# First loads and projections reordered, and every fourth head of layer 0 masked behind its exponentials by GpSimd, in a two-layer gated attention kernel

## What is computed

```python
scores = jnp.einsum('bhqd,bhkd->bhqk', Q, K) / scale
scores = jnp.where(mask, scores, NEG_INF)          # -1e10
attention = jax.nn.softmax(scores, axis=-1)
heads_out = jnp.einsum('bhqk,bhkd->bhqd', attention, V)
```

## Time and profile before

| | |
|---|---|
| median of 3 runs | 1293.08 us (1290.47 to 1293.56) |
| the profiled execution's own time | 1296.06 us |
| its span, first to last instruction | 1294.8 us |
| mean granted TensorE clock | 0.984 of full |
| TensorE busy | 1212.6 us |
| VectorE busy | 894.7 us |
| ScalarE busy | 710.4 us |
| GpSimd busy | 480.4 us |

### The profile page before, as it was taken

One profiled execution on the slowest core, in us unless ns is written; L12 is line 12 of the kernel. 1 busy time (PEld: TensorE's weight loads), 2 busy tenths in 40 slices (PEclk: granted clock), 3 DMA queues, 4 the chain that ended last, 5 costly groups with the idle time before them and its releaser, 6 DMA issues.

```text
span 1294.8 us, 25126 instructions
## 1 busy us (share of the span) xinstructions
PE 1212.6 (94%) x9236; PEld 858.0 (66%) x9236; DVE 894.7 (69%) x2680; ACT 710.4 (55%) x1197; POOL 480.4 (37%) x675
## 2 busy tenths in 40 slices
PE   6799999999999989999999989999999999888998
PEld 5466667666776664444448866676676776577987
DVE  2678767886777646589999956767868777642333
ACT  1355555555655548889983326666566665622221
POOL 5344333443343100057000434343643643322555
PEclk8899999999999999999999999999999999988999
DMA  5422334233432032000003644364464342137983
GB/s 158 140 79 82 109 92 128 80 87 107 121 104 67 11 97 84 1 1 1 1 1 124 198 138 116 99 161 136 135 170 123 117 137 61 51 144 230 312 198 39
DMA packets 121941, 137.22 MB, mean 106 GB/s; under 512 B 12881, under 2 KB 116427, under 8 KB 121797
## 3 DMA queue, kind: packets, MB, share of 16 engines
q1 hardware_dynamic: 111888, 125.98, 32.9%
q0 software_dynamic: 7296, 8.15, 3.5%
q10 hardware_dynamic: 2634, 1.49, 0.4%
HBM read 58.42 MB, written 27.36 MB: 66 GB/s over the span
## 4 chain that ended last, share of the span: by engine, by line
PE 56%; DVE 6%; issue 3%; ACT 2%; DMA 1%; POOL 1%; SPq 1%; ACTq 0%; POOLq 0%; DVEq 0%
PE PS L641 14%; PE PS L687 5%; PE PS L444 5%; PE PS L384 5%; PE PS L427 4%; PE PS L655 4%; PE PS L403 4%; PE PS L502 2%; PE PS L696 2%; PE PS L476 2%; PE PS L391 2%; DVE NM L1086 1%; PE PS L520 1%; PE PS L485 1%; ACT P L808 1%
## 5 line engine op out<-in xcount | busy, mean ns | idle before, releaser
L808 ACT ACTIVATE P<-PS 128x512 f32<-128x512 f32 x512 | 302.2, 601 | 165.0 <-PE PS L430 98.3
L1083 DVE CUSTOM_DVE_ANT_0 MX<-PS,NQ 128x256 bf16<-128x256 f32 x512 | 192.5, 418 | 66.9 <-PE PS L403 66.6
L427 PE MATMUL PS<-QS,KS 99*128 99x256 bf16 x1024 | 225.7, 274 | 8.1 <-ACT P L808 7.1
L1086 DVE TENSOR_REDUCE NM<-PS 128x2 f32<-128x512 f32 x256 | 173.6, 685 | 75.9 <-PE PS L403 71.4
L403 PE MATMUL PS<-KS,QS 96*128 96x256 bf16 x1024 | 196.8, 275 | 23.4 <-DVE NM L1083 15.1
L403 PEld LDWEIGHTS PS<-KS,QS 96*128 96x128 bf16 x1024 | 87.0, 98 | 89.0 <-DVE NM L1083 28.2
L444 PE MATMUL PS<-P,V 128*32 128x256 f32 x2048 | 137.0, 385 | 1.5 <-ACT P L808 1.5
L427 PEld LDWEIGHTS PS<-QS,KS 99*128 99x128 bf16 x1024 | 95.2, 99 | 53.9 <-ACT P L808 20.5
L430 PE MATMUL PS<-NK,identb 128*128 128x256 bf16 x512 | 126.9, 273 | 0.0
L641 PE MATMUL PS<-XNT,wup 128*128 128x512 f16 x576 | 124.9, 379 | 0.0
L641 PEld LDWEIGHTS PS<-XNT,wup 128*128 128x128 f16 x576 | 56.2, 98 | 67.4
(11 more groups left out here) (233 smaller groups left out, 2476.1 us busy)
## 6 DMA issues: line engine op xcount, KB each, us to landing
KS<-PP SPq DMA_DIRECT2D x192, 128.0 KB, 2.9
QS<-PP SPq DMA_DIRECT2D x192, 128.0 KB, 2.4
WH<-in_wex SPq DMA_DIRECT2D x16, 768.0 KB
WG<-in_wex SPq DMA_DIRECT2D x10, 768.0 KB
bufd<-bias_row SPq DMA_DIRECT2D x5, 1032.0 KB, 12.2
XB<-in_x SPq DMA_DIRECT2D x16, 256.0 KB, 2.9
CT<-in_ctxT SPq DMA_DIRECT2D x16, 256.0 KB, 3.1
x1d<-XB SPq DMA_DIRECT2D x16, 256.0 KB, 2.1
```

The lines of the kernel that those rows point to most:

```text
L427: ins = tensor.matmul(o, t.KS[b % 3][0:99, h, 128 * kt:128 * kt + 128], t.QS[b % 3][0:99, h, :], start=True, stop=(L == 1))
L808: scalar.activation(t.P[h % 8][:, :, :], PS[:, h % 2, :].rearrange("p (k n) -> p k n", k=2), ACT.Exp).then_inc(s_ex, 1)
L1083: ins = vector.tensor_tensor_reduce(t.MX[:, 2 * (h % 2) + qt, :], PS[:, bk, 256 * qt:256 * qt + 256], t.NQ[b % 4][:, qt, :], -1.0, 1.0e30, ...
L1086: ins = vector.tensor_reduce(nm[:, :, h], PS[:, bk, :].rearrange("p (t n) -> p t n", t=2), X, ALU.max, negate=True)
```

## The change

Masking. In layer 0 heads 0, 4, 8 and 12 no longer get the penalty matmuls on their transposed scores. Instead `pe_marks` sums the penalties NK of all keys by a matmul with ones, `dve_marks` makes from this and the mask bytes a tile MK of ones and zeros (ones where a key counts, and for a query that has none), and `pool_mask` on GpSimd limits the exponentials to 1 and multiplies them with MK, at slots 1, 7, 9 and 13. `pe_av` waits for it (s_pm). There are three buffers MK; loading a mask also waits for the marks of the batch before the last.

First loads. SyncE issues rows, mask and context of batches 0 and 1 and rows and mask of batch 2 in one burst; the context of batch 2 comes at (-2, 14). Norms of batches 0 and 1 both run in s = -3. Batch 0's rows are transposed before its keys are projected. The casts and low pieces of batch 1's queries move from the sixth to the ninth slot of its head work, their stacks behind them. Twelve warming matmuls stand before the values of batch 0. ScalarE's bias loads and rows of ones come at (-1, 0), GpSimd's gated biases and the bias additions of batches 0 and 1 at (-1, 5) and (-1, 6), its clearing of V before the first slot.

Beside these, semaphores are merged (s_z and s_num into s_iv, d_cr into d_i, d_wr into d_ql) and w_r lies in unused columns of AM. The diff, cut to its core:

```diff
@@ -126,6 +126,18 @@
+def masked_after(L, h):
+    return L == 0 and h % 4 == 0
+def mark_at(s, k):
+    if (s, k) == (-3, 5):
+        return 0
+    return s + 2 if k == 14 and 1 <= s + 2 < NB else None
@@ -134,6 +146,32 @@
+def norms_at(L, s, k):
+    if s == -3:
+        steps = [(0, k + 6)] + ([(1, k + 3)] if L == 0 else [])
+    else:
+        steps = [(s + 3, k)] if s + 3 < NB and (L, s) != (0, -2) else []
+    return [(b, kk) for b, kk in steps if 6 <= kk <= 10]
+def loads_at(L, s, k):
+    return k == 2 and (L, s) not in ((0, -2), (0, -1))
+def mid_at(L, b):
+    return 8 if (L, b) == (0, 1) else 5
+def rows_first(L, b):
+    return (L, b) == (0, 0)
@@ -233,7 +272,7 @@
         w_s = tile(m, "w_s", [128, 48], F32)
-        w_r = tile(m, "w_r", [128, 48], F32)
+        w_r = AM[:, 48:96]
@@ -416,17 +456,18 @@
         def pe_scores_t(L, b, h):
...
             i = 16 * n + h
-            pe.wait_ge(d_i, 48 * (L + 1))
+            pe.wait_ge(d_i, 16 + 48 * (L + 1))
...
             pe.wait_ge(s_ex, i - 1)
-            if L == 0:
+            if L == 0 and not masked_after(L, h):
...
                 o = PS[:, bk, 256 * kt:256 * kt + 256]
+                on_scores = L == 0 and not masked_after(L, h)
                 ins = tensor.matmul(o, t.KS[b % 3][0:99, h, 128 * kt:128 * kt + 128], t.QS[b % 3][0:99, h, :],
-                                    start=True, stop=(L == 1))
-                if L == 0:
+                                    start=True, stop=not on_scores)
+                if on_scores:
@@ -436,6 +477,8 @@
             pe.wait_ge(s_ex, 16 * n + 4 * g + 4)
+            if L == 0:
+                pe.wait_ge(s_pm, 4 * b + g + 1)
@@ -445,6 +488,15 @@
+        def pe_marks(b):
+            bk = odd_bank(("mk", b), s_mk, b + 1)
+            pe.wait_ge(s_cst, 1)
+            pe.wait_ge(s_pen, b + 1)
+            for kt in range(2):
+                ins = tensor.matmul(PS[:, bk, 0:256], onesb[:, :], t0.NK[b % 4][:, kt, :], start=(kt == 0), stop=(kt == 1))
+            ins.then_inc(s_mc, 1)
@@ -547,13 +599,15 @@
                     continue
+                if kk == (0 if rows_first(L, b) else 1):
+                    pe_xn(L, b)
...
                     pe_keys(L, b)
-                if kk == 1:
-                    pe_xn(L, b)
...
                 if kk == 13:
+                    if (L, b) == (0, 0):
+                        pe_warm(5, 12)
@@ -577,6 +631,8 @@
                     pe_ranks(GROUP_OF[s - 2][0])
+            if L == 0 and mark_at(s, k) is not None:
+                pe_marks(mark_at(s, k))
@@ -782,21 +838,24 @@
+        def spread(v, n):
+            return v.rearrange("(o n) -> o n", o=1).broadcast_to([128, n])
+        def act_biases():
+            scalar.dma_start(bias_row[:, 0, :], spread(a["b0"], D)).then_inc(s_g, 16)
+            scalar.dma_start(bias_row[:, 1, :], spread(a["b1"], D)).then_inc(s_g, 16)
         def act_setup():
-            def spread(v, n):
-                return v.rearrange("(o n) -> o n", o=1).broadcast_to([128, n])
...
             scalar.dma_start(gates[:, 2:4], spread(a["g_ffn"], 2)).then_inc(s_g, 16)
-            scalar.dma_start(bias_row[:, 0, :], spread(a["b0"], D)).then_inc(s_g, 16)
-            scalar.dma_start(bias_row[:, 1, :], spread(a["b1"], D)).then_inc(s_g, 16)
-            act.wait_ge(s_g, 64)
+            act.wait_ge(s_g, 32)
...
             act.wait_ge(s_cr, 1)
-            scalar.dma_start(crd, XNf[0:3, 0:2048]).then_inc(d_cr, 16)
+            scalar.dma_start(crd, XNf[0:3, 0:2048]).then_inc(d_i, 16)
         def act_ones(L):
-            act.wait_ge(d_cr, 16)
+            act.wait_ge(d_i, 16)
@@ -904,10 +963,10 @@
                     continue
+                if kk == (0 if rows_first(L, b) else 1):
+                    act_xt(L, b)
...
                     act_split(L, b, 0)
-                if kk == 1:
-                    act_xt(L, b)
@@ -1010,8 +1069,10 @@
         def act_program():
             act_setup()
-            act_ones(0)
             for s, k in slots(0):
+                if (s, k) == (-1, 0):
+                    act_biases()
+                    act_ones(0)
@@ -1091,6 +1152,13 @@
+        def dve_marks(b):
+            dve.wait_ge(s_mc, b + 1)
+            dve.wait_ge(s_pm, 4 * (b - 2))
+            vector.scalar_tensor_tensor(t0.MK[b % 3][:, :, :], bc(PS[:, home["mk", b], 0:256], 1, 2), (S - 0.5) * NEG,
+                                        t0.MM[b % 2][:, 2:4, :], ALU.is_le, ALU.max).then_inc(s_mk, 1)
@@ -1285,12 +1353,16 @@
         def dve_slot(L, s, k):
...
                 dve_max(L, s + 1, h)
+            if L == 0 and (s, k) == (-3, 6):
+                dve_marks(0)
+            if L == 0 and k == 0 and 1 <= s + 1 < NB:
+                dve_marks(s + 1)
...
                     dve_mid(L, b, 0)
-                if kk == 5:
+                if kk == mid_at(L, b):
@@ -1315,12 +1387,11 @@
                         dve_route_slots(GROUP_OF[s - 2][0])
-            if 0 <= s + 3 < NB:
-                kk = k if s > -3 else k + 6
+            for b, kk in norms_at(L, s, k):
                 if L == 0 and kk == 6:
-                    dve_any(s + 3)
-                if 7 <= kk <= 10:
-                    dve_head_norm(L, s + 3, kk)
+                    dve_any(b)
+                if kk >= 7:
+                    dve_head_norm(L, b, kk)
@@ -1578,12 +1649,23 @@
+        def pool_mask(b, h):
+            pool.wait_ge(s_mk, b + 1)
+            pool.wait_ge(s_ex, 16 * b + h + 1)
+            p = t0.P[h % 8][:, :, :]
+            gpsimd.tensor_scalar(p, p, 1.0, None, ALU.min).then_inc(*pool.tick())
+            pool.wait_ge(*pool.last())
+            gpsimd.tensor_tensor(p, p, t0.MK[b % 3][:, :, :], ALU.mult).then_inc(s_pm, 1)
         def pool_masks(b):
...
             pool.wait_ge(s_st, 16 * (b - 3))
+            pool.wait_ge(s_mc, b - 3)
@@ -1655,6 +1737,8 @@
         def pool_slot(L, s, k):
+            if L == 0 and 0 <= s < NB and k in (1, 7, 9, 13):
+                pool_mask(s, {1: 0, 7: 4, 9: 8, 13: 12}[k])
@@ -1663,16 +1747,17 @@
                     pool_rest(L, b, int(kk == 3))
-                if kk in (2, 5):
-                    pool_low(L, b, int(kk == 5))
+                if kk in (2, mid_at(L, b)):
+                    pool_low(L, b, int(kk > 2))
...
                     pool_masks(s + 3)
+            for b, kk in norms_at(L, s, k):
                 if kk == 8:
-                    pool_rstd(L, s + 3)
-                if kk == 10:
-                    pool_bias(L, s + 3)
+                    pool_rstd(L, b)
+                if kk == 10 and (L == 1 or b >= 2):
+                    pool_bias(L, b)
@@ -1691,14 +1776,16 @@
         def pool_program():
             pool_setup()
+            for i in range(3):
+                pool_values(0, i)
             for s, k in slots(0):
-                if (s, k) == (-3, 4):
+                pool_slot(0, s, k)
+                if (s, k) == (-1, 5):
                     pool_biases()
-                pool_slot(0, s, k)
-                if (s, k) == (-2, 2):
-                    for i in range(3):
-                        pool_values(0, i)
-            gpsimd.memset(bias_row[:, :, :].rearrange("p i n -> p (i n)")[:, 0:D + 2], 0.0).then_inc(s_z, 1)
+                    pool_bias(0, 0)
+                if (s, k) == (-1, 6):
+                    pool_bias(0, 1)
+            gpsimd.memset(bias_row[:, :, :].rearrange("p i n -> p (i n)")[:, 0:D + 2], 0.0).then_inc(s_iv, 1)
@@ -1731,6 +1818,7 @@
         def sp_load_mask(b):
...
             sp.wait_ge(s_av, b - 1)
+            sp.wait_ge(s_mk, b - 1)
@@ -1809,24 +1897,37 @@
         def sp_slot(L, s, k):
-            if s == -3 and k == 0:
+            if (L, s, k) == (0, -3, 0):
+                for b in range(2):
+                    sp_load_rows(L, b)
+                    sp_load_mask(b)
+                    if b == 0:
+                        sp_weight(L, "k")
+                    sp_load_ctx(L, b)
+                    if b == 0:
+                        sp_weight(L, "q")
+                sp_weight(L, "v")
+                sp_load_rows(L, 2)
+                sp_load_mask(2)
+                sp_weight(L, "o")
+            if (L, s, k) == (1, -3, 0):
                 sp_load_rows(L, 0)
-                if L == 0:
-                    sp_load_mask(0)
...
                     sp_weight(L, n)
-            if 0 < s + 3 < NB and k == 2:
+            if 0 < s + 3 < NB and loads_at(L, s, k):
...
                     sp_load_mask(s + 3)
+            if (L, s, k) == (0, -2, 14):
+                sp_load_ctx(L, 2)
...
                         sp_stack(L, b, 0, part)
-                    if kk == (4, 6, 6)[part]:
+                    if kk == (4, mid_at(L, b) + 1, mid_at(L, b) + 1)[part]:
```

More of the change, by code:

```diff
@@ L217, in late_tiles @@
                 t.NK = [tile(m, f"NK{i}", [128, 2, 256], BF16) for i in range(4)]
+                t.MK = [tile(m, f"MK{i}", [128, 2, 256], BF16) for i in range(3)]
         top0 = ExitStack()
@@ L304, in build @@
         TL = (t0, t1)
```

(9 more changed lines are left out.)

12 lines of the change are left out of this document (6 added, 6 removed).

## The result

The changed kernel takes **1320.74 us** (median of 4 runs, 1319.59 to 1324.25) against 1293.32 for the kernel before beside it (4 runs, 1290.47 to 1295.31): ratio 1.0218, 95% interval 1.019 to 1.0247. It is slower by 27 us. The prediction, 1287.4 and at most 1298.0, was wrong, in its sign too. The profiled execution took 1319.59 us, its span is 1318.2.

What follows compares the result with a forecast made beforehand. TensorE, 94% busy, was taken as the bound. Terms -10.6 + 17.0 - 3.1 - 9.0 = -5.7 us took the profiled 1296.06 to 1290.4; with the median 3 us lower, the forecast was 1287.4 us, range 1274 to 1298.

Steps and rivals of the forecast that it cites:

- The step that failed: GpSimd's limit to 1, priced from another row at 0.62 us, upper end 0.96, which would add 4.4 us in all.
- part 3: Masking on GpSimd: a limit and multiply pair of 1.87 us, late for head 4; net of stalls +13.9 us.
- part 1: Mask matmuls on TensorE in layer 0: 128 fewer at 0.11 us, -14.1, two marks matmuls a batch +3.5; together -10.6 us.
- part 4: The reordered start: first maximum at about 27.0 us, first transposed score at 44.5 instead of 53.54; -9.0 us.
- Rival B: The start does not pay, gaining 2 us instead of 9: 1294.4 us, chance 0.16.
- The head-4 stall: TensorE waits at the second AV group for GpSimd's masking: +17.0 us, less 3.1 of waits for maxima.
- part 2: Marks on VectorE: one 128x512 operation a batch at slot 0, 0.69 us, hidden in waits for scores, costed at nothing.
- Rival C: VectorE's casts and norms held up behind GpSimd's masking, half of 2.8 us a batch reaching TensorE: 1310 us, chance 0.14.

Runs made afterwards that it cites:

- e1: Changed kernel with all masking back on TensorE, no marks and no GpSimd masking, only the reordered start left: 1286.28 us, ratio 0.9951 to the kernel before.
- e13: Changed kernel with the four heads' mask matmuls left out and nothing in their place, no marks, those heads unmasked: 1282.51 us, ratio 0.9932 to the kernel before.
- e14: Changed kernel without masking of the four heads, but with the marks made and read by nobody: 1282.44 us, ratio 0.9927 to the kernel before.
- e12: Changed kernel with a two-operation limit and masking at slots 1, 6, 9 and 13: 1286.73 us, ratio 0.9961 to the kernel before.
- e9: Changed kernel with one edit, the limit naming a second operation (min 1.0, max 0.0), at the old slots: 1299.72 us, ratio 1.0057 to the kernel before.
- e4: Changed kernel with eight warming matmuls ahead of the second AV group in batches 0 to 12: 1316.3 us, ratio 1.0174 to the kernel before.
- e10: Changed kernel with a two-operation limit and masking at slots 1, 5, 9 and 15: 1293.74 us, ratio 1.0013 to the kernel before.
- e11: Changed kernel with a two-operation limit and masking at slots 1, 5, 10 and 15: 1292.58 us, ratio 1.0006 to the kernel before.

## Why the prediction was wrong

The runs make a ladder from the kernel before to the changed one: start alone -6.0 (e1), matmuls out -3.8 (e13), marks 0 (e14), masking of the short kind and well placed +4.3 (e12), head 4 at slot 7 instead of 6 +13.0 (e9), the long limit +21.0: 1292.3 + 28.5 = 1320.8. The prediction had -5.7 where this has +28.5. Of the 34.2 us between, 21.0 are the limit, 6.8 the matmuls with the marks, 3.0 the start, and 3.4 the masking with the short limit (17.3 for 13.9). (The error itself is 33.3: the kernel before stands at 1292.3 here and at 1293.1 in the forecast.) The prediction's steps against it:

- **The step that failed** is in part 3: "I take 0.62, since that row has the same width and constants", with 0.96 as upper end. It was 1.49. The pair became 2.75 for 1.87 us, each stall of head 4 grew by 0.87, and with what follows from it (e9) that made 21.0 us: nearly two thirds of the error of 33. It is not all of it: with the pair as assumed the kernel takes 1299.7, still slower than before and above the range. The prediction had priced the upper bound at +4.4 us, and even 0.87 a batch by its own working would have been +11.3. Both rows with constants that it took as neighbours, L1585 and L1550, name two operations in the code; the limit names one. I compared widths and constants and overlooked the form.
- **The mask matmuls** (part 1, -10.6) gave -3.8 with the marks. "TensorE waits little", and from it "So there a matmul taken away is time", was the wrong reading of the earlier trace rows. Each slot ends at one of two engines, 0.2 to 0.3 us apart: the earlier trace rows show the score of 227.88 already waiting 0.28 us for a maximum. A matmul is gain only in the segments with no such wait, one in four here. This was a second miss, 6.8 us.
- **The start** (part 4, -9.0) was right in its steps: 26.71 for 27.0, 45.85 for 44.5. In e1 it is -8.75 at the first transposed score, -7.9 at the first AV group, -6.8 at the last (batch 3 loses 0.9, 8.41 us from first to second group for 7.54) and -6.0 in the medians: 3 us less than counted. Both losses stand beside a stretch at 1.2 GHz (49.6 to 53.0 and 134.9 to 138.3 us) that the kernel before doesn't have. Rival B is refuted.
- **The head-4 stall** (part 3, +17.0 - 3.1) was right in place and order: 14 waits in the changed kernel's steady part and 12 in e9's, all at the second AV group. Head 12's lateness in the last two batches wasn't foreseen. With the pair of 1.87 us TensorE's stall for head 4 is 12.9 us (e9), for 17.0: in batch 6 it is 1.12, not 1.41. The waits for maxima behind it are gone, as counted. Moving the masking ahead of the penalties gives 13.0 us back (e12).
- **The clock behind the stalls** is not in the prediction, which put it at nothing: 7.6 us in the changed kernel (e4) and 5.6 in e9. Its sum came near e9's all the same, 13.9 for 17.3, in part by luck: the stall was counted too long, the clock and VectorE's held steps not at all.
- **Marks on VectorE** (part 2) took 0.68 us, hidden, as e14 shows.
- **Rival C** (VectorE held behind GpSimd) gave 1310 and a chance of 0.14. Its mechanism is real: casts of 0.42 last up to 1.41 us, norm steps up to 1.23. Its price is less than feared: at most 4.3 us in e12, about 1 of it head 12's lateness in the last two batches, and 6 more where the cast of slot 5 is hit (e10, e11). The Trainium skill, GPSIMD Engine Reference, Key points, says that GpSimd shares its SBUF interfaces with VectorE; the trace agrees for casts and norm steps (their ends lie 0.28 and 0.15 us behind the multiply's). The maxima, which read PSUM and write bf16, kept their 0.42 us, and 1310 came from assuming that half of the held time, 1.4 us a batch, reaches TensorE: e12 has 0.27 a batch at most.

What is not shown: why a limit with one operation takes longer, whether another single operation does, and how it is on other engines or widths; and why some waits are followed by 1.2 GHz and others of the same length are not. The ladder's steps were each measured at one place in it; in another order they could divide the sum otherwise.

## What to carry to other kernels

Price a new operation by a row with the same form, not only the same shape: count its operands and operations, and where no row has them, let the upper bound go well past the nearest. Before a matmul is counted as gain, look slot by slot at who ends last; in a pipeline where two engines finish within 0.3 us of each other only the slots without that wait pay. A masking moved by one slot (7 to 6, past two small operations in GpSimd's order) was worth 13 us, 5.6 of them slow clock: what matters is the order in the queue and what stands in it ahead, not the slot's number.
